# Waits that other waits imply are left out of a tile pipeline, z gets ten buffers, and ScalarE's steps of a tile change places

## The reference, cut to what matters

```python
h = einsum('td,edf->etf', xt, W1) + b1          # F = 512
h = layernorm(relu(h), g1, be1)
y = einsum('etf,efd->etd', h, W2) + b2          # D = 128
y = layernorm(relu(y), g2, be2)
out = einsum('te,etd->td', gate, y)             # gate: 2 of 8 experts, shares add to 1
```

## Time and profile before

| What | Before |
|---|---|
| median of three runs | 324.51 us |
| profiled execution | 324.29 us |
| its span | 322.7 us |
| PE busy | 254.7 us (79%), 2960 matmuls |
| DVE busy | 232.2 us (72%) |
| ACT busy | 211.9 us (66%) |
| POOL busy | 190.3 us (59%) |

### The profile page before, as it was taken

How to read it: one execution, slowest core, us unless ns; L and a number is a source line. 1 busy time by engine, 2 the same in 40 slices (tenths; PEclk the granted TensorE clock), 3 DMA queues, 4 the chain that set the end, 5 groups by cost and what they waited for, 6 DMA issues and landing times.

```text
span 322.7 us, 10282 instructions
## 1 busy us (share of the span) xinstructions
PE 254.7 (79%) x2960; PEld 201.9 (63%) x2960; DVE 232.2 (72%) x1091; ACT 211.9 (66%) x795; POOL 190.3 (59%) x300
## 2 busy tenths in 40 slices
PE   3997547899385738758977889998889888899995
PEld 3455445556273715237866787997789787788631
DVE  1789648343476385667876778898799888889975
ACT  2467445628282739716776788797799788789830
POOL 9403728562717073738566766686668666677660
PEclk9999859579859596859999999999999999999999
DMA  6994941211311311435231222332223555541337
GB/s 182 351 286 138 289 162 44 69 56 43 122 37 58 106 51 59 98 70 129 64 76 52 61 60 66 66 62 63 62 63 87 148 141 134 117 117 29 101 123 242
DMA packets 48675, 34.56 MB, mean 107 GB/s; under 512 B 26870, under 2 KB 42742, under 8 KB 48619
## 3 DMA queue, kind: packets, MB, share of 16 engines
q1 hardware_dynamic: 38972, 22.80, 25.7%
q0 software_dynamic: 6592, 9.00, 9.8%
q10 hardware_dynamic: 3056, 2.11, 2.1%
HBM read 15.11 MB, written 12.02 MB: 84 GB/s over the span
## 4 chain that ended last, share of the span: by engine, by line
PE 31%; ACT 18%; another core or an unknown queue 17%; issue 17%; DVE 13%; DVEq 1%; DMA 1%; ACTq 1%
PE bank L721 19%; PE bank L725 11%; ACT rh L1353 2%; DVE kq L1894 2%; ACT cxT L1376 2%; ACT ex L1181 2%; ACT vv L1365 2%; DVE vo L1901 2%; ACT xt L1204 1%; ACT rg L1388 1%; ACT square_mask L1360 1%; DMA wr<-in_L_ffn_Wr 1%; DVE cx L1931 1%; ACT xT L1128 1%
## 5 line engine op out<-in xcount | busy, mean ns | idle before, releaser
L667 POOL DMA_INDIRECT slot_rows<-pay,pos x64 | 65.1, 1017 | 61.3 <-DVE pay L1765 44.3
L679 POOL DMA_INDIRECT answers<-vo,words_of x71 | 70.7, 995 | 43.0 <-ACT vo L1395 29.9
L1353 ACT ACTIVATE rh<-bank 128x512 f16<-128x512 f32 x71 | 41.5, 585 | 26.2 <-remote 21.7
L721 PE MATMUL bank<-kb_room,w1h 128*128 128x128 f16 x568 | 56.3, 220 | 0.8 <-issue 0.7
L725 PE MATMUL bank<-w2h,rh 128*128 x284 | 51.6, 219 | 3.1 <-ACT rh L1353 2.5
L725 PE MATMUL bank<-rh 128*128 128x129 f16 x284 | 51.7, 220 | 1.0 <-issue 0.9
L721 PE MATMUL bank<-kb_room,w1l 128*128 128x128 f16 x284 | 51.6, 220 | 0.4 <-issue 0.3
L725 PE MATMUL bank<-w2l,rh 128*128 x284 | 51.5, 219 | 0.5 <-issue 0.5
L725 PE MATMUL bank<-w2h,kq 128*128 x284 | 40.5, 222 | 11.2 <-DVE kq L1894 8.0
L1894 DVE SCALAR_TENSOR_TENSOR kq<-bank,rh 128x512 f16<-128x512 f32 x71 | 47.9, 675 | 0.5 <-ACT rh L1353 0.4
L1901 DVE CUSTOM_DVE_ANT_0 vo<-bank,square_mask 128x257 f32<-128x257 f32 x71 | 29.9, 421 | 23.8 <-ACT square_mask L1360 22.1
(11 more groups left out here) (259 smaller groups left out, 635.7 us busy)
## 6 DMA issues: line engine op xcount, KB each, us to landing
x_tok<-in_x SPq DMA_DIRECT2D x8, 256.0 KB, 7.1
w1f<-in_L_ffn_W SPq DMA_DIRECT2D x2, 1024.0 KB, 9.3
pay<-pay SPq DMA_DIRECT2D x8, 256.0 KB
w1f<-answers SPq DMA_DIRECT2D x8, 256.0 KB
w2f<-answers SPq DMA_DIRECT2D x8, 256.0 KB, 2.9
kb_room<-slot_rows SPq DMA_TRANSPOSE x71
words_of<-slot_rows POOLq DMA_DIRECT2D x71, 1.0 KB
answers<-vo,words_of POOLq DMA_INDIRECT x71
```

The costliest lines, as they stand in the source:

```text
L667: eng.indirect_dma_start(slot_words, bass.IndirectOffsetOnAxis(ap=pos[:, g % 2, k, i:i + 1], axis=0), pay[g % 2][:, k, i, :].bitcast(U32), ...
L679: eng.indirect_dma_start(answers, bass.IndirectOffsetOnAxis(ap=words_of[:, j % NW, 0:1], axis=0), z[j % NZ], None).then_inc(s_ans[j % NZ], 16)
L721: return eng.matmul(dst, lhsT, rhs, start=start, stop=stop)
L1353: eng.activation(rh_all(j), psH[j % 3][:, :].rearrange("p (c n) -> p c n", c=FC), ACT.Relu).then_inc(s_rh, 1)
```

## The change

It does four things. (1) It takes out second waits that another wait already implies: five on ScalarE (`relu1`, `sum_`, `std1`, `relu2`, `std2`), four on VectorE (`r_lo`, `square_sums`, `affine`, `aggr2`) and two in `roots`, which keeps one. (2) z gets 10 places in place of 5, and `words_of` 10 in place of 12; so `scaled` no longer waits for an answer to land, while GpSimd waits for that in `words` (now for the answer ten tiles back, before twelve) and, in the last five tiles, in `answer`. (3) `gate_share` keeps its wait for `s_rs` and `gained` its wait for `s_z` only in the last two or three tiles. (4) ScalarE's order in a slot is now relu1, sum_, std2, relu2, gate_share, std1, scaled; before it was relu1, sum_, std2, gate_share, relu2, scaled, std1.

```diff
-        NW, NS, LEAD = 12, 8, 2
+        NW, NS, LEAD = 2 * NZ, 8, 2
-        z = [vo_all[:, n * D:(n + 1) * D] for n in range(3, 3 + NZ)]
+        z = [vo_all[:, n * D:(n + 1) * D] for n in range(3, 3 + NZ)] + [cx[:, n, :] for n in range(3, 3 + NW - NZ)]
...
             def answer(j):
                 eng.wait_ge(s_z, j + 1)
+                if j + NZ >= SLOT_TILES:
+                    eng.wait_ge(s_ans[j % NZ], answered(j - NZ))
...
-                    z[j % NZ], None).then_inc(s_ans[j % NZ], 16)
+                    z[j % NW], None).then_inc(s_ans[j % NZ], 16)
...
             def relu1(j):
-                if j >= 3:
-                    eng.wait_ge(p_y, j - 2)
...
             def sum_(j):
-                if j >= 2:
-                    eng.wait_ge(s_s2, j - 1)
...
             def std1(j):
-                if j >= 4:
-                    eng.wait_ge(s_rs, rooted(j - 2))
...
             def relu2(j):
-                if j >= 3:
-                    eng.wait_ge(s_w, j - 2)
...
             def std2(j):
-                if j >= 2:
-                    eng.wait_ge(s_rs, rooted(j))
...
             def gate_share(j):
-                eng.wait_ge(s_rs, rooted(j + LAG2))
+                if j + LAG2 - LAG1 >= SLOT_TILES:
+                    eng.wait_ge(s_rs, rooted(j + LAG2))
...
             def scaled(j):
-                if j >= NZ:
-                    eng.wait_ge(s_ans[j % NZ], answered(j - NZ))
-                eng.activation(z[j % NZ], w_[j % 3], ACT.Copy, scale=rg[j % 4][:, :]).then_inc(s_z, 1)
+                eng.activation(z[j % NW], w_[j % 3], ACT.Copy, scale=rg[j % 4][:, :]).then_inc(s_z, 1)
...
-                if 0 <= p - 4 < SLOT_TILES:
-                    gate_share(p - 4)
                 if 0 <= p - 2 < SLOT_TILES:
                     relu2(p - 2)
                 if 0 <= p - 4 < SLOT_TILES:
-                    scaled(p - 4)
+                    gate_share(p - 4)
                 if 0 <= p - 1 < SLOT_TILES:
                     std1(p - 1)
+                if 0 <= p - 4 < SLOT_TILES:
+                    scaled(p - 4)
...
             def r_lo(j):
-                if j >= 2:
-                    eng.wait_ge(p_y, j - 1)
...
             def square_sums(j):
-                if j >= 4:
-                    eng.wait_ge(s_vv, j - 3)
...
             def affine(j):
-                if j >= 3:
-                    eng.wait_ge(s_ur, j - 2)
...
             def aggr2(j):
-                if j >= 4:
-                    eng.wait_ge(s_std2, j - 3)
...
             def gained(j):
-                if j >= 3:
+                if j + LAG2 - 1 >= SLOT_TILES:
                     eng.wait_ge(s_z, j - 2)
...
             def roots(p):
-                if p >= LAG2:
+                else:
                     eng.wait_ge(s_std2, p - LAG2 + 1)
-                if p >= LAG2 + 4:
-                    eng.wait_ge(s_z, p - LAG2 - 3)
```

## The result

The changed kernel takes 313.55 us (median of 4 runs, 311.85 to 314.87), the kernel before in the same session 324.14 us (4 runs, 322.89 to 324.84). The ratio is 0.967, 95% interval 0.961 to 0.974: 10.6 us faster. The profiled executions have 311.85 us (span 310.2) and 324.29 us (span 322.7). The prediction was 324.6, its range ended at 320.4.

What follows compares the result with a forecast made beforehand. It took VectorE to set undisturbed slots at 1.86 us, PE and ScalarE close behind, with late TensorE counts lengthening others. Terms 0 - 0.1 - 0.1 + 0.4 = +0.2 us gave 324.5 profiled, 324.7 on the median, stated 324.6; range 320.4 to 327.2.

Steps and rivals of the forecast that it cites:

- The two kinds of slots: In the loop: undisturbed slots of 1.86 us set by VectorE, and longer disturbed ones in which a TensorE count comes late.
- The term of late counts: Late TensorE counts in the loop, 13 VectorE waits of 1.35 us each, 17.6 in total: taken as unchanged.
- Fewer late counts: Rival, in the loop: ScalarE's shift changes how often TensorE's counts come late; two fewer, 1.35 us each, 321.9 us; chance 0.13.
- Part 1, the waits: Waits removed on ScalarE and VectorE: taken as 0, at most 3.4 us gained, plus 0.1 from instruction-stream holes.
- the only hole of their size: VectorE's 0.18 us idle ahead of one affine, unexplained by semaphores; a shorter stream might save 0 to 0.2, taken 0.1.
- PE's 1.80: PE's 32 matmuls need 1.80 us a slot; rival that waits cost VectorE time: slots fall to this, 321.1 us, chance 0.20.
- Part 2, ten places for z: scaled no longer waits for an answer to land: gain 0.1 us from 0 to 0.2; the waits moved to GpSimd cost 0.
- Part 3, the order: ScalarE's new order: earlier relu2 and std1 gain 0, but relu2 waits 0.11 us for affine; cost 0.4 us, 0 to 1.4.
- The ring: Loop from square_sums through affine, relu2, relu1 and sum_ back: 1.88 us a tile, before 1.79; rival 325.7 us, chance 0.20.
- The resets: A late count about every fourth slot puts ScalarE ahead again, which could bring part 3's cost from 1.4 us down to 0.
- The sum: Whole kernel: 0 - 0.1 - 0.1 + 0.4 = +0.2 us on the profiled 324.29, forecast 324.6.

Runs made afterwards that it cites:

- p3h: Kernel before with plain loads, waits out and ten places for z, old order: 266.16 us, ratio 0.990 to the kernel before.
- s3: Kernel before with plain loads, waits out and ten places for z, old order, on another chip: 269.18 us beside 268.31 for the kernel before.
- p1h: The whole change with plain loads (transposition left out): 267.95 us, ratio 0.996 to the kernel before.
- p2h: Kernel before with plain loads and ScalarE's new order alone, all waits kept: 269.72 us, ratio 1.000 to the kernel before.
- s1: The whole change with plain loads, on another chip: 270.03 us (two runs) beside 268.31 for the kernel before.
- s2: Kernel before with plain loads and ScalarE's new order alone, on another chip: 269.29 us, ratio 1.010 to the kernel before.
- r2: Kernel before with plain loads, waits out, ten places for z, and only relu2 moved ahead of gate_share: 275.09 us, ratio 1.016.
- u1: Kernel before with plain loads, in a session with late counts: 307.07 us beside 323.55 for the kernel before, ratio 0.951.
- u2: Kernel before with plain loads and ScalarE's new order alone, in a session with late counts: 309.79 us beside 323.55 for the kernel before.
- u3: Kernel before with plain loads, waits out and ten places for z, old order, in a session with late counts: 305.28 us beside 323.55.
- p0h: Kernel before with plain loads and nothing else changed: 268.52 us, ratio 0.997 to the kernel before.

## Why the prediction was wrong

**What bounds the kernel.** The two kinds of slots were read rightly, and so was the mechanism of the disturbed one: relu1 late, sum_ behind it, square_sums behind that. The step that failed is the sentence that closed it: "neither the order nor the waits of TensorE are in the change". From that I kept the number of late counts as it was in the forecast and moved it by two in the rivals. But the counts did change, though not one instruction of TensorE did. The term of late counts was 0 in the sum; it measured -14.1 us (the slots longer than 2 us), with VectorE's long waits for sum_ going from 13 to 2. "Fewer late counts" was the right rival with a sound price, 1.35 us each: 11 fewer would have been -14.9. It had 0.13, and two of thirteen as its size, with nothing behind the two. The earlier trace rows had one group that was 17.6 us large and of unknown cause; a forecast whose range lets such a group change by 2.7 us claims to know more about it than it does.

**Part 1, the waits, taken as 0.** About right for the cost that was argued. 476 instructions fewer on ScalarE and 407 on VectorE (and 5 more on GpSimd) are the seven and six of a tile. The earlier trace rows are not the only hole of their size either: the waits before have one of 0.2 us at square_sums too. Neither moves the sum. Without late counts the slot stays 1.855 with the waits out (p3h, s3); VectorE does not fall to PE's 1.80. The ratio of p3h, 0.990 (0.984 to 0.996), hints at a gain, that of s3, 1.000 (0.992 to 1.008), doesn't. Whether the 878 instructions fewer are what makes counts late less often beside transposing loads is open.

**Part 2, ten places for z.** Nothing contradicts the -0.1. The answer landed in time: 298.92 to 301.93 is 3.0 us, against 3.6 in the earlier trace rows, and the gather starts 4.4 us ahead of the end of PE's run (301.93 and 306.37; before it was 4.0). What follows PE's run takes 3.8 us until the end of the span in both.

**Part 3, the order, taken as +0.4 of at most +1.4.** The mechanism was right and the size too small. The ring was put at 1.88 us a tile and measured 1.889 (p1h), 1.888 (p2h, s1) and 1.887 (s2), so +1.3 to +1.5 us on the loop: the upper end, not the middle. The resets that I set against it don't come where no count is late. In the changed kernel with its transposing loads it is 1.902 to 1.909, more than 1.889. What adds to it, as far as the traces show, are slots in which relu1 waits a little for `p_h`: 18, 13 and 17 slots of the three traces are 1.95 to 2.2 us long, against 1 in p1h. In one of them relu1 starts 0.44 us behind scaled instead of 0.29, as `p_h` rises at 227.97, 0.59 behind its matmul:

```profile
227.55 0.39 ACT L1386 ACTIVATE vo<-cx,rg 128x128 f32<-128x128 f32 x1
227.99 0.60 ACT L1353 ACTIVATE rh<-bank 128x512 f16<-128x512 f32 x1
```

The working of part 3 had one hole that didn't matter here: a step that reads the result of the step ahead of it in its own queue has a spacing of its own (0.31 for 0.20 in r2). "With each step's spacing as now" holds only while the neighbours' dependencies stay apart.

**The sum.** -14.1 for late counts, some +2.4 for longer undisturbed slots and -0.7 ahead of the loop make -12.4; the spans differ by 12.5. The -0.7 is within what that start does by itself: it moves between 143.70 and 147.42 us over the seven traces of such sessions.

**What stays open.** Why TensorE's counts come late, what differs between the sessions, which part of the change makes the late counts rare, and by what mechanism; what is shown is that they are rarer, and that this is the gain. To tell the parts apart needs the order and the waits alone, with transposing loads, in such a session; with plain loads there are too few late counts for it (3 slots in each of u1, u2 and u3). Of the two, waits and z alone in the old order would be the version to test first, by the slots of p3h, s3 and u3. Also not run: the changed kernel with transposing loads in a session at 269 us.

## What to carry to other kernels

- When one group of waits of unknown cause is larger than everything else in the sum, its change is the forecast's uncertainty. Put it into the range in full, both ways, and don't argue it constant because the change doesn't name its engine.
- Before a gain is credited to an edit, run the edit's parts and the kernel before where the disturbance is absent. Here the change gains 10 us with it and, on plain loads, nothing without it, and one part of it, the new order, costs 1.3 to 1.5 us of the loop where no count is late.
- In a queue that is nearly full, order steps so that no step reads the one directly ahead of it, and check each moved step for its own input, not only for those who wait for it.

## What the runs showed of the hardware

- The same program on the same chip takes 269 us in one session and 324 in another, steadily within each (265.69 to 273.55 in the four sessions of the one kind, 320.69 to 328.99 in the three of the other). The difference starts in the first 100 us, and 37 us of it lie ahead of the loop (u1 against p0h).
- A count of TensorE came 0.23 to 0.24 us behind the start of the matmul that raised it, each time that it can be matched, in thirteen traces of the one kind; in the seven of the other, medians are 0.23 to 0.73 us, with single counts over 3 us.
- Transposing loads of 71 tiles, against plain ones, cost the kernel before nothing that can be measured in the one kind (0.4 us) and 16.5 us in the other, where its profile has 15 slots over 3 us with them (first session) and 3 without (u1). It isn't the loads' own landing: in the trace before, no engine waits for a tile's rows in the loop.
- An ACTIVATE that reads the 128x1 result of the one directly ahead of it starts 0.03 us behind its end: 0.31 us from start to start behind gate_share (0.28 long, r2), 0.22 behind vv (0.19 long, and r2). One that doesn't read it overlaps it and starts 0.18 to 0.20 behind its start.
